# Self-attention of a decoder layer: a new order of its rounds, and its operands loaded by 5 transfers a step instead of 16

## The reference, cut to what matters

```python
x = x + attn(layernorm(x))          # 16 heads of 16, causal, batch 4, 512 tokens
# inside attn, xn = second layernorm with gamma, beta
q = (xn @ Wq.T + bq) / 4            # k, v alike without the factor
s = q @ k.T + M @ rel_bias[h] @ M.T # M interpolates 32 bias rows to 512
s = where(mask_upper_triangle, -inf, s)
out = softmax(s) @ v                # then @ Wo.T + bo
```

## Time and profile before

| | us |
|---|---|
| median of 3 runs (2820.21 to 2823.96) | 2821.69 |
| the profiled execution's own time | 2821.53 |
| its span, first to last instruction | 2819.7 |
| busy in the span: PE, PEld | 2608.1, 2328.3 |
| busy in the span: DVE, ACT, POOL | 1967.0, 1594.1, 132.6 |
| mean granted TensorE clock | 0.972 of full |
| `self_projections` | 0 to 83.9 |
| `self_attention`, first product to last store | 112.7 to 442.6 |

### The profile page before, as it was taken

The page is one execution under the profiler, slowest core; times in us unless marked ns, Lnnn a source line. Parts: engine busy times, 40 slices in busy tenths (PEclk is TensorE's granted clock), DMA queues, the critical chain, the costliest instruction groups (busy, mean ns, idle before and its releaser), DMA issues. The chain is left out here.

```text
span 2819.7 us, 47515 instructions
## 1 busy us (share of the span) xinstructions
PE 2608.1 (92%) x17664; PEld 2328.3 (83%) x17664; DVE 1967.0 (70%) x3680; ACT 1594.1 (57%) x3005; POOL 132.6 (5%) x153
## 2 busy tenths in 40 slices
PE   6477777799999999999999999999999999999976
PEld 4466666599989988998899889988998899889975
DVE  6366667577767777776777677767776777677776
ACT  4366662366656664665565655655565566556644
POOL 0450002100000000000000000000000000000003
PEclk9799999799999999999999999999999999999987
DMA  5563321500030002001100120011001100110000
GB/s 177 166 166 80 81 53 51 192 23 15 16 113 16 23 28 93 20 18 55 66 24 15 61 68 16 15 60 68 16 15 60 68 16 23 53 63 23 8 12 30
DMA packets 94881, 152.85 MB, mean 54 GB/s; under 512 B 48400, under 2 KB 62096, under 8 KB 93680
## 3 DMA queue, kind: packets, MB, share of 16 engines
q1 hardware_dynamic: 90176, 137.48, 15.3%
q0 software_dynamic: 3200, 12.59, 1.3%
q10 hardware_dynamic: 1328, 0.39, 0.1%
HBM read 123.02 MB, written 23.20 MB: 52 GB/s over the span
## 5 line engine op out<-in xcount | busy, mean ns | idle before, releaser
L1292 ACT CAST pt_hi<-xt_ps 128x512 fp32r<-128x512 f32 x1024 | 592.5, 585 | 574.9 <-PE xt_ps L1262 558.9
L1358 DVE TENSOR_TENSOR pt_lo<-xt_ps,pt_hi 128x512 fp32r<-128x512 f32 x1024 | 704.7, 688 | 265.3 <-ACT pt_hi L1292 262.1
L1347 DVE TENSOR_SCALAR_CACHE_REDUCE xprobs<-xs_ps 128x1024 f32<-128x1024 f32 x512 | 626.7, 1224 | 175.3 <-PE xs_ps L1211 170.5
L1273 PE MATMUL xo_ps<-pt_hi,v_hi 128*128 128x256 f32 x2048 | 649.5, 317 | 1.3 <-DVE pt_lo L1358 1.3
L1298 ACT ACTIVATE xprobs<-xprobs,xneg_max 128x1024 f32<-128x1024 f32 x512 | 591.5, 1155 | 26.7 <-DVE xneg_max L1353 26.7
L1262 PE MATMUL xt_ps<-ident,xprobs 128*128 128x128 f32 x4096 | 604.2, 272 | 0.0
L1273 PE MATMUL xo_ps<-pt_lo,v_hi 128*128 128x256 f32 x2048 | 577.6, 282 | 0.0
L1273 PE MATMUL xo_ps<-pt_hi,v_lo 128*128 128x256 f32 x2048 | 576.1, 281 | 0.0
L1262 PEld LDWEIGHTS xt_ps<-ident,xprobs 128*128 128x128 f32 x4096 | 485.0, 140 | 60.7 <-issue 6.9
L1273 PEld LDWEIGHTS xo_ps<-pt_hi,v_hi 128*128 128x128 f32 x2048 | 388.8, 190 | 4.0 <-DVE pt_lo L1358 1.3
L1273 PEld LDWEIGHTS xo_ps<-pt_lo,v_hi 128*128 128x128 f32 x2048 | 389.4, 190 | 1.9
(11 more groups left out here) (203 smaller groups left out, 2842.4 us busy)
## 6 DMA issues: line engine op xcount, KB each, us to landing
blocks<-ctx_split SPq DMA_DIRECT2D x68, 768.0 KB, 5.7
xq<-x_split SPq DMA_DIRECT2D x64, 512.0 KB, 3.2
q_st<-rel_split SPq DMA_DIRECT2D x64, 128.0 KB, 2.5
q_st<-q_split SPq DMA_DIRECT2D x192, 32.0 KB, 2.0
k_st<-k_split SPq DMA_DIRECT2D x192, 32.0 KB, 1.9
ctx_split<-ctx_out POOLq DMA_DIRECT2D x8, 768.0 KB, 4.3
v_st<-v_split SPq DMA_DIRECT2D x64, 64.0 KB, 2.3
x_split<-xq_out SPq DMA_DIRECT2D x8, 512.0 KB, 4.8
```

The source lines that it names most:

```text
L1273: last = pe.matmul(o_ps[:, 0:GQ], v[:, vs], pt[:, c % 3, GQ * j:GQ * (j + 1)], start=c == 0 and j == 0 and m == 0, stop=c == PIECES - 1 an ...
L1292: act.copy(pt_hi[:, c % 3, :], t_ps[:, c % 3, :]).then_inc(t_rounded, 1)
L1347: dve.tensor_scalar(probs[:, par if kind == "A" else 1 - par, t, CHUNK * i:CHUNK * (i + 1)], s_ps[:, buf, :], LOGIT, None, ALU.mult, ALU.m ...
L1358: dve.tensor_tensor(pt_lo[:, c % 3, :], t_ps[:, c % 3, :], pt_hi[:, c % 3, :].bitcast(F32), ALU.subtract).then_inc(t_ready, 1)
```

## The change

In DRAM q and k get a layout of (channel, 3, token), in which the three rows of a channel are the ones that the stack wants: hi, hi, lo for q, hi, lo, hi for k. So hi is stored twice: six stores of 1 MB for q and six for k in place of four each, and the waits count three. In SBUF the stacks and the values become one tensor each (four slots of a pair of heads, two slots of values), so that one transfer brings the bias rows of both heads, one q, one k, and two the values: 5 a step. The eight loads of `key_split` become one that repeats its source. SP loads the stacks of steps 0 and 1, the values of 0 and 1, then the stacks of 2 and 3; in the loop `load_v` comes before `load_stacks`. The orders of TensorE, ACT and DVE in the loop are new, in single rounds (`ROUND_OF`); the first two steps are filled by the same loop, begun at n = -2 or -3, with the work of absent steps skipped. The work per step, its shapes and its semaphores are otherwise the same.

```diff
-        q_split = nc.dram_tensor("q_split", (2, C, T), F32).ap()
-        k_split = nc.dram_tensor("k_split", (2, C, T), F32).ap()
+        q_split = nc.dram_tensor("q_split", (C, 3, T), F32).ap()
+        k_split = nc.dram_tensor("k_split", (C, 3, T), F32).ap()
...
-                for w, dest in enumerate((q_split, k_split)):
+                for w, (dest, hi_at, lo_at) in enumerate(((q_split, (0, 1), 2), (k_split, (0, 2), 1))):
                     n += TB
                     sp.wait_ge(stage_hi_ready, n)
-                    sp.dma_start(dest[0, rows], stage_hi[:, w, :].bitcast(F32)).then_inc(stack_stored[w], 16)
+                    for j in hi_at:
+                        sp.dma_start(dest[rows, j, :], stage_hi[:, w, :].bitcast(F32)).then_inc(stack_stored[w], 16)
                     sp.wait_ge(stage_lo_ready, n)
-                    sp.dma_start(dest[1, rows], stage_lo[:, w, :].bitcast(F32)).then_inc(stack_stored[w], 16)
+                    sp.dma_start(dest[rows, lo_at, :], stage_lo[:, w, :].bitcast(F32)).then_inc(stack_stored[w], 16)
             sp.wait_ge(key_stored, 16)
             for w in range(2):
-                sp.wait_ge(stack_stored[w], 16 * 2 * CH)
+                sp.wait_ge(stack_stored[w], 16 * 3 * CH)
...
-                    dve.wait_ge(stack_stored[w], 16 * 2)
+                    dve.wait_ge(stack_stored[w], 16 * 3)
...
-                    act.wait_ge(stack_stored[w], 16 * 2)
+                    act.wait_ge(stack_stored[w], 16 * 3)
...
-        q_st = [sb(f"q_st{s}", [STACK, N], F32R) for s in range(8)]
-        k_st = [sb(f"k_st{s}", [STACK, N], F32R) for s in range(8)]
-        v_st = [sb(f"v_st{s}", [P, QI, P], F32R) for s in range(4)]
+        q_st, k_st = sb("q_st", [STACK, 4, 2, N], F32R), sb("k_st", [STACK, 4, 2, N], F32R)
+
+        v_st = sb("v_st", [P, 2, 2 * V_SPAN], F32R)
...
+        ROUND_OF = ((0, (0,)), (0, (1,)), (1, (0,)), (1, (1,)), (2, (0, 1)))
+        ROUNDS = len(ROUND_OF)
...
             def load_stacks(n):
-                cols = slice(N * (n // PAIRS), N * (n // PAIRS + 1))
-                for h, s, _ in heads(n):
-                    rows = slice(SD * h, SD * (h + 1))
-                    sp.dma_start(q_st[s][0:REL_ROWS, :].bitcast(F32), rel_split[h]).then_inc(stack_loaded[s], 16)
-                    for stack, split, parts in ((q_st, q_split, (0, 0, 1)), (k_st, k_split, (0, 1, 0))):
-                        for j, part in enumerate(parts):
-                            at = REL_ROWS + SD * j
-                            sp.dma_start(stack[s][at:at + SD, :].bitcast(F32), split[part, rows, cols]).then_inc(stack_loaded[s], 16)
+                p, b, u = n % PAIRS, n // PAIRS, n % 4
+                cols = slice(N * b, N * (b + 1))
+                rows = slice(2 * SD * p, 2 * SD * (p + 1))
+                sp.dma_start(q_st[0:REL_ROWS, u].bitcast(F32),
+                             rel_split[2 * p:2 * p + 2].rearrange("k r n -> r k n")).then_inc(stack_loaded[u], 16)
+                for stack, split in ((q_st, q_split), (k_st, k_split)):
+                    sp.dma_start(stack[REL_ROWS:, u].bitcast(F32),
+                                 split[rows, :, cols].rearrange("(k d) j n -> (d j) k n", k=2)).then_inc(stack_loaded[u], 16)
 
             def load_v(n):
-                b = n // PAIRS
-                for k, (h, _, s) in enumerate(heads(n)):
-                    at = PAIR_ROWS * k
-                    sp.dma_start(v_st[s][:, :, at:at + SLOT_ROWS].bitcast(F32),
-                                 v_split[:, QI * b:QI * (b + 1), SLOT_ROWS * h:SLOT_ROWS * (h + 1)].bitcast(F32)).then_inc(v_loaded[s], 16)
-
-            for s in range(8):
-                sp.dma_start(k_st[s][0:REL_ROWS, :].bitcast(F32), key_split).then_inc(keys_loaded, 16)
-                if s % 2:
-                    load_stacks(s // 2)
+                p, b, u = n % PAIRS, n // PAIRS, n % 2
+                for k in range(2):
+                    at = SLOT_ROWS * (2 * p + k)
+                    sp.dma_start(v_slots(u)[:, k, :, 0:SLOT_ROWS].bitcast(F32),
+                                 v_split[:, QI * b:QI * (b + 1), at:at + SLOT_ROWS].bitcast(F32)).then_inc(v_loaded[u], 16)
+
+            sp.dma_start(k_st[0:REL_ROWS].rearrange("r u k n -> r (u k) n").bitcast(F32),
+                         key_split.rearrange("r (a n) -> r a n", a=1).to_broadcast([REL_ROWS, 8, N])).then_inc(keys_loaded, 16)
+            for n in range(2):
+                load_stacks(n)
             sp.wait_ge(v_padded, 1)
             for n in range(2):
                 load_v(n)
+            for n in range(2, 4):
+                load_stacks(n)
             for n in range(STEPS):
+                if 2 <= n + 1 < STEPS:
+                    sp.wait_ge(weighed, n)
+                    load_v(n + 1)
                 if n + 4 < STEPS:
                     sp.wait_ge(scored, 3 * n + 3)
                     load_stacks(n + 4)
-                if 2 <= n + 1 < STEPS:
-                    sp.wait_ge(weighed, n)
-                    load_v(n + 1)
...
-            for s in range(4):
-                pool.memset(v_st[s][:].bitcast(F32), 0.0).then_inc(pool_self, 1)
-            pool.wait_ge(pool_self, 4)
-            for s in range(4):
-                at = PAIR_ROWS * (s % 2) + SLOT_ROWS
-                last = pool.memset(v_st[s][:, :, at:at + 1].bitcast(F32), 1.0)
+            for u in range(2):
+                pool.memset(v_st[:, u].bitcast(F32), 0.0).then_inc(pool_self, 1)
+            pool.wait_ge(pool_self, 2)
+            for u in range(2):
+                last = pool.memset(v_slots(u)[:, :, :, SLOT_ROWS:SLOT_ROWS + 1].bitcast(F32), 1.0)
...
-                for k, (_, s, _) in enumerate(heads(n)):
-                    if u == 0:
-                        pe.wait_ge(stack_loaded[s], LOADS * (n // 4 + 1))
+                if u == 0:
+                    pe.wait_ge(stack_loaded[n % 4], LOADS * (n // 4 + 1))
+                for k in range(2):
...
-                for k, (_, _, s) in enumerate(heads(n)):
-                    if c == 0:
-                        pe.wait_ge(v_loaded[s], 16 * (n // 2 + 1))
-                        if k == 0 and n >= 1:
-                            pe.wait_ge(attn_stored, n)
-                    m = 5 * n + bank_of(k, c)
-                    pe.wait_ge(pt_ready, m + 1)
+                m = ROUNDS * n + r
+                c, ks = ROUND_OF[r]
+                if r == 0 and n >= 1:
+                    pe.wait_ge(attn_stored, n)
+                if r == 0:
+                    pe.wait_ge(v_loaded[n % 2], 16 * 2 * (n // 2 + 1))
+                pe.wait_ge(pt_ready, m + 1)
...
             pe.wait_ge(const_ready, 1)
-            pe.wait_ge(keys_loaded, 16 * 8)
-            for u in range(3):
-                scores(0, u)
-            scores(1, 0)
-            for n in range(STEPS):
-                scores(n + 1, 1)
-                turn(n, 0, [0])
-                turn(n, 0, [1])
-                weigh(n - 1, 2)
-                scores(n + 1, 2)
-                weigh(n, 0)
-                turn(n, 1, [0])
-                turn(n, 1, [1])
+            pe.wait_ge(keys_loaded, 16)
+            for n in range(-2, STEPS):
+                turn(n, 4)
+                weigh(n, 1)
+                weigh(n, 2)
                 scores(n + 2, 0)
-                weigh(n, 1)
-                turn(n, 2, [0, 1])
-            weigh(STEPS - 1, 2)
+                turn(n + 1, 0)
+                turn(n + 1, 1)
+                scores(n + 2, 1)
+                weigh(n, 3)
+                weigh(n, 4)
+                turn(n + 1, 2)
+                scores(n + 2, 2)
+                turn(n + 1, 3)
+                weigh(n + 1, 0)
...
             act.copy(ident_r[:], ident[:]).then_inc(const_ready, 1)
-            for u in range(3):
-                exponents(0, u)
-            for n in range(STEPS):
-                exponents(n + 1, 0)
-                round_turned(5 * n)
-                store(n - 1)
-                round_turned(5 * n + 1)
-                exponents(n + 1, 1)
-                round_turned(5 * n + 2)
-                round_turned(5 * n + 3)
-                exponents(n + 1, 2)
-                round_turned(5 * n + 4)
-            store(STEPS - 1)
+            for n in range(-2, STEPS):
+                round_turned(n, 4)
+                round_turned(n + 1, 0)
+                round_turned(n + 1, 1)
+                exponents(n + 2, 0)
+                store(n)
+                round_turned(n + 1, 2)
+                exponents(n + 2, 1)
+                round_turned(n + 1, 3)
+                exponents(n + 2, 2)
...
-            for u in range(3):
-                maxima(0, u)
-            maxima(1, 0)
-            for n in range(STEPS):
-                maxima(n + 1, 1)
-                rest_of_turned(5 * n)
-                rest_of_turned(5 * n + 1)
-                maxima(n + 1, 2)
-                rest_of_turned(5 * n + 2)
-                maxima(n + 2, 0)
-                rest_of_turned(5 * n + 3)
```

(89 more changed lines are left out.)

## The result

| | before | changed |
|---|---|---|
| median, us (range, runs) | 2820.95 (2817.42 to 2823.96, 4) | 2714.78 (2713.35 to 2715.54, 4) |
| the profiled execution, its span | 2821.53, 2819.7 | 2713.35, 2711.5 |
| TensorE busy, PE and PEld | 2608.1, 2328.3 | 2578.7, 2320.1 |
| mean granted clock | 0.972 | 0.979 |

The ratio is 0.9623, with a 95% interval of 0.9607 to 0.964: 106 us, 3.8% faster. The forecast was 2718; the measured time is 3 us under it, inside the likeliest case's range of 2703 to 2743.

What follows compares the result with a forecast made beforehand. The written order of TensorE's rounds was taken to bound the attention loop, with SP's queue close behind. The terms -87.5 - 1.8 - 19.2 + 5.2 = -103.3 against 2821.5 gave 2718 us, range 2703 to 2758.

Steps and rivals of the forecast that it cites:

- the likeliest case: Whole kernel: the change works as forecast, at a period of 6.8 to 7.7 us, total 2703 to 2743; chance 0.73.
- The written order bound the loop: Attention loop: TensorE asks rounds back before ACT and DVE can have handled them, 3.05 us of waits in a 9.82 us step.
- SP was close behind: SP's queue in the attention loop: issues take about 8.8 us a step, so a better order alone could not go under 8.8.
- The loop through ACT: Attention step: the longest loop between TensorE's turned rounds and ACT's work on them takes 7.02 us, equal to TensorE's own 7.0.
- The term of the sum: Attention stage from first turned round to last store: new order of rounds takes 232.8 us in place of 320.3, gain 87.5.
- The start: SP's first load to TensorE's first product: fewer transfers cut 28.75 us to 9.5, gain 19.2, from 15 to 22.
- The stores: Projections before the attention stage: 4 MB of added stores lengthen ACT's wait; cost 5.2 us, low 2.6, high 10.3.
- Rounds that close in part: Rival, attention loop: work on DVE or ACT slips each step; period 8.2 to 8.4, total 2753 to 2760; chance 0.17.
- a start that gains alone: Rival: the order returns what it takes, the period stays 9.8 us and only the stage's start gains, 2807; chance 0.05.
- a slower loop: Rival, attention loop: TensorE waits for ACT, whose loop becomes the bound; with 11 us a step, 2845; chance 0.04.
- E2: ACT's 128x256 unit in the attention step, 0.86 us; TensorE's first round of that step cannot be turned before it.
- The clock rival: A fuller TensorE is throttled more; dips three times more often add some 10 us, within the range; chance 0.01 for more.

Runs made afterwards that it cites:

- the keys by slot: Changed kernel with its one load of `key_split` cut into four, each issued just ahead of its step's stacks: 2711.03 us, ratio 0.961 against the kernel before.
- with six stores: Kernel before with only the three-row DRAM layouts and so six stores each for q and k; its 16 loads and orders stay: 2826.54 us, ratio 1.0024.
- with four stores: Changed kernel with the old DRAM layouts, so four stores each for q and k, and 9 transfers a step: 2712.89 us, ratio 0.9619 against the kernel before.
- both variants: Changed kernel with four stores, 9 transfers a step and `key_split` loaded in four parts ahead of their stacks: 2706.06 us, run again 2707.03 us.

## Why the prediction was right, point by point

*The written order bound the loop.* Shown from both sides. The old orders with idle loads keep the 3.0 us of waits and 9.77; the new ones bring 7.02. A period down by 9.82 - 7.02 = 2.80 answers to PEld's 3.05 us of waits, less the 0.24 that came anew, and not to the 2.1 in which PE was idle and by which the period would be 7.7. In this the trace agrees with the Trainium skill (Perfetto Trace Analysis, Identifying the Most-Contended Engine), by which matmul busy time is the poorer measure. The orders of the three engines were only put back together, so how the gain divides among them is not shown.

*SP was close behind.* The bound of 8.8 from the earlier trace rows was real and a little low: 9.1 measured. The two parts together gain 106 us, alone 13.6 and 45.3; the other 47 are had only with both. Both single parts hold the earlier first product, though, 9 us each. From the first turned round to the last store the kernel before takes 320.3 us, the old orders with the new loads 314.0, the new orders with 16 transfers 285.9 and both together 225.6: of the 94.7 us, 54 are had only with both.

*The loop through ACT, 7.02.* Its length was right and so is its place: 0.40 us added in it costs 0.38, added beside it nothing. Two details differ. TensorE's own work was laid out at 7.0 us, equal to the loop; it is 6.8, so the loop alone sets the period. And R2 starts at 247.94, when the store of 247.45 lets it, 0.69 after T2 at 247.25 in place of 0.63: the store, released by W4, now stands in the loop, by less than 0.1 us.

The term of the sum was mis-sized all the same, 7.2 us too small a gain. The margin for slips, 7.1 in place of 7.0, was not needed: 31 x 0.08 = 2.5 us. "I keep 5 us" of half-clock stretches was the other step that failed: none came. The first rounds at half clock took little: T4(0), at 114.81, comes 5.2 us after T0(0), where 4.8 + 1.5 was forecast, 1.1 too much. Against these stand a step that is 1.0 longer (its wait for values at 185) and an end that saves 1.5 and not 2.

*The start, 19.2 forecast, 16.2 found.* The step that failed is the rate, 282 GB/s in the earlier trace rows. It was read as that of loads ahead of the stage, but in that window only one third of the bytes are SP's loads (q1). Two thirds are those of POOL's queue (q0), a 768 KB store of context among them that was issued at 97.75 and landed 4.5 us later (the kernel before, transfers of 100 to 105 us: packets, MB, share):

```profile
DMA packets 599, 1.41 MB, mean 282 GB/s; under 512 B 174, under 2 KB 174, under 8 KB 599
q0 software_dynamic: 260, 0.94, 59.2%
q1 hardware_dynamic: 339, 0.47, 40.5%
```

With the new loads the engines were as full and moved 218 GB/s, and from SP's first load to the first product 2.55 MB in 12.52 us, while the forecast had counted the 1.7 MB needed and at worst 0.5 of context ahead of it: some loads of the next steps ran among them. The order of SP's queue was part of it too: 1 MB of keys for four steps stood ahead of the first stacks, and the keys by slot bring 12.5 to 9.4 us. Why loads move less than that mix was not taken apart. In a second execution the changed kernel needed 13.9 us, so this term's error is 3.0 to 4.4 us.

*The stores, 5.2 forecast.* 5.4 in the trace, 7.3 alone (4.2 to 9.6). The timeline shows that ACT's wait for k's stores grew from the 2.94 us of the earlier trace rows:

```profile
69.04 2.42 ACT L352 ACTIVATE stage_hi<-banks,bqk_scaled 128x512 fp32r<-128x512 f32 x4 [5.85 <-DMA k_split<-stage_lo]
```

It ends 5.7 us later than at 63.33. The last two of the four megabytes lie beside v's projection, as argued: from the end of that wait to SP's first load it is 20.3 us now and was 20.6.

*The rivals.* Rounds that close in part, a start that gains alone and a slower loop are all ruled out by 7.02 us a step and one wait of 1.1. The last came nearest: T0 does wait for E2, 0.24 us a step. The clock rival went the other way.

*The sum.* That the total came within 3 us of the forecast (5 by the two traces, 108.2 against 103.3) is in part luck: a loop 7.2 us shorter and a start 3.0 us longer than forecast have opposite signs.

*The half-clock stretches.* The mean granted clock over the loop is 0.98 before and with six stores, 0.99 with the old orders or with four stores, 0.93 with the new orders and 16 transfers, and 1.00 in the changed kernel and in the other variants. It looks as if TensorE's long waits go with it: up to 4.1 us in the kernel at 0.93, 2.8 right before the stretch of the one with four stores. But the old orders with the new loads wait 3.0 us a step, as the kernel before does, and have one stretch instead of four, and the second execution with both variants waits 2.1 us once and stays at 1.00. What decides is open.

## What to carry to other kernels

Lay a proposed order out on the busiest engine with each unit as long as it occupies it, then close every loop through the other engines: the longest was right to 0.1 us. Ask what stands next behind the wait that is removed; here the two gain 106 us together, and the new order with the queue behind it full gains 45. And merge transfers no further than the queue needs: four stores and nine loads, with the first step's operands in front, are 6.8 us faster than six stores and five.

## What the runs showed that was not expected

Full DMA engines move very different amounts: 408 GB/s in stores and 282 in a mix of a store and loads before, 218 and 201 in loads at the starts of two new kernels. And in the steady steps a transfer over more rows is hardly dearer to issue, as one step on SP's queue in the changed kernel shows (timeline): 128 rows of values 0.65 each, 64 rows of two heads 0.64, 48 of two heads 0.59 and 0.43, against 0.45 to 0.50 for the 16-row ones above.

```profile
240.42 1.29 SPq L475 DMA_DIRECT2D v_st<-v_split  x2
241.75 0.64 SPq L465 DMA_DIRECT2D q_st<-rel_split  x1
242.43 0.59 SPq L468 DMA_DIRECT2D q_st<-q_split  x1
243.07 0.43 SPq L468 DMA_DIRECT2D k_st<-k_split  x1
```

That holds while the DMA engines have room, at a share of 0.55 here. With them full, at the start of the same stage, a single issue took over 5 us (timeline; it costs nothing, since what it loads is for the third step):

```profile
99.94 5.36 SPq L465 DMA_DIRECT2D q_st<-rel_split  x1
```
